# Routed experts on the rows that chose them, in tiles of 128 rows, instead of every expert on every row

## The chip, the cores and the metric

One core of one Trainium2 chip. The metric is the device time of one execution in microseconds (us), median of three runs. TensorE is PE in the rows below, VectorE is DVE, ScalarE ACT, GpSimd POOL, SyncE SP.

## What is computed

One transformer layer on x of 4 x 2048 rows of 256 numbers, all fp32: layer norm with modulation, a delta-rule attention with convolutions and a learned mix of three branches, then the expert layer that the change is about. Only the last part of the reference matters here:

```
scores = jax.nn.sigmoid(x @ gate_weight.T)             # 16 experts in 4 groups
...                                                    # best 2 groups, then the best 4 experts of a row
combine = jnp.zeros((T, E), jnp.float32).at[jnp.arange(T)[:, None], topk_idx].add(topk_w)
up = jnp.einsum('th,ehi->eti', x, expert_up)           # 256 -> 128, per expert
down = jnp.einsum('eti,eih->eth', jax.nn.silu(up), expert_down)
moe_out = jnp.einsum('te,eth->th', combine, down)
shared = jax.nn.silu(x @ shared_up) @ shared_down      # 256 -> 512 -> 256
return (moe_out + shared).reshape(B, S, H)
```

12 of a row's 16 weights in `combine` are zero.

## The kernel before

The program runs seven stages one after the other, each a block of its own on all engines: setup, norm_inputs, conv_heads, long_filter, chunk_inverses, delta_scan and mix_and_experts. Only the last one is changed in substance (L1462 to L2082). It takes 16 units of 512 rows (UT; J = 4 pieces of 128 rows; UB = 4 units to a batch element).

For each unit there are two kinds of work. `mix(u, i, s)` has 40 numbered steps s on every engine: statistics of the three branches (DVE, s 0 and 1, L1873; POOL takes the square roots as powers, L1655), the router network (PE s 7 to 15, L1697 to L1718; ACT gelu L1805), softmax (s 15 to 17), the weighted sum of the branches (DVE L1922 to L1934, POOL L1660 and L1663), its rms (ACT L1812, DVE L1937, POOL L1666, DVE L1943), the output projection (PE s 29 and 30, L1725 and L1732), the residual x2 (DVE L1952), its layer norm (L1958 to L1968, POOL L1668), transposes and modulation to h2T (PE L1740, ACT L1826), and the gate logits (PE s 38, L1746; ACT exp L1831). `route` (DVE, four parts, L1979 to L2044) makes the weights `comb` from them. Each step waits for the one before it, mostly on another engine, so a unit's mix is one chain.

The expert part has NX = 20 slots per unit: 4 pieces of the shared expert and 16 routed experts. In a slot PE does `up` (L1755, two matmuls of 512 columns), ACT the silu (L1838), PE `down` (L1769, four matmuls of 256 columns), and DVE adds the result times its weight into `acc` (L2060). All 16 experts run on all rows, whatever the weights; their up and down weights stay in SBUF (`eup`, `edn`).

`units_ahead` (L240) orders it: `front` runs the mix of unit 0 alone, then each `body` of unit u writes its 20 slots and the mix of unit u+1 interleaved, two steps a slot, in the same fixed order on every engine. The bodies are a hardware loop over three batch elements and a tail. Every engine is in order. The mix inputs vf, fl, dl, x and hT are double buffered and loaded on SP's queue; POOL closes a unit with `finish` (L1673, L1676), and SP stores it.

An fp32 matmul stands twice in the trace (x8 for four matmuls).

## Time and profile before

| what | value |
|---|---|
| median of three runs | 3187.55 us (3185.85 to 3205.73) |
| the profiled execution | 3187.41 us, span 3185.6 us |
| PE busy in the span | 88% |
| DVE, ACT, POOL busy | 52%, 34%, 19% |
| granted PE clock, mean | 0.817 of 2.4 GHz |
| bytes moved by DMA | 269.81 MB, 85 GB/s |

Busy is the time in which an engine had an instruction under way; it says nothing of what would be late next if that engine were faster. The granted clock is 1.00 at 2.4 GHz and 0.50 at 1.2 GHz; a value between is a mean over a stretch. The span is the first to the last instruction; the time of the execution is 1.8 us longer.

### The profile page before, as it was taken

What the parts mean: (1) busy time and instruction counts of PE and PEld (TensorE: products, weight loads), DVE (VectorE), ACT (ScalarE), POOL (GpSimd) and SP (SyncE); (2) the same over time, 40 slices, a digit from 0 to 9 for tenths busy, and PEclk for the clock granted to TensorE, in tenths of its full rate; (3) what the DMA queues carried; (4) which work ended last, traced back from release to release, by engine and by line L of the source; (5) the groups of instructions that cost most, each with busy time, mean ns of one, the idle gap of its engine ahead of it and who ended that gap; (6) DMA issues with size and microseconds to landing.
All of it is one profiled execution on the core that took longest, in us unless ns stands there. A gap on an engine that the chain in (4) does not pass through costs nothing.

```text
span 3185.6 us, 39962 instructions
## 1 busy us (share of the span) xinstructions
PE 2801.9 (88%) x13712; PEld 2052.0 (64%) x13712; DVE 1650.9 (52%) x4322; ACT 1076.5 (34%) x2142; POOL 618.1 (19%) x417
## 2 busy tenths in 40 slices
PE   4989994444998799999569999999999999999998
PEld 4966663333888678788446666666666666666665
DVE  3448883218142233333246665675656756667655
ACT  1258774233543111111123333323333233333231
POOL 1115552021100100000122122221222212222201
PEclk7579997665555666665679999999999999999999
DMA  3425557765663433434410011110111101111000
GB/s 97 139 93 164 162 172 194 184 131 129 148 140 103 136 108 109 129 87 129 159 40 19 29 47 47 48 47 1 47 47 48 47 1 47 47 47 47 7 1 14
DMA packets 348447, 269.81 MB, mean 85 GB/s; under 512 B 166284, under 2 KB 305996, under 8 KB 346724
## 3 DMA queue, kind: packets, MB, share of 16 engines
q1 hardware_dynamic: 337680, 256.90, 27.9%
q0 software_dynamic: 2304, 8.39, 1.0%
q10 hardware_dynamic: 8276, 2.10, 0.3%
q8 instruction: 108, 1.77, 0.2%
q14 instruction: 79, 0.65, 0.1%
HBM read 166.45 MB, written 100.89 MB: 84 GB/s over the span
## 4 chain that ended last, share of the span: by engine, by line
PE 35%; DVE 7%; POOL 6%; issue 2%; SPq 0%; DMA 0%; ACT 0%; POOLq 0%; DVEq 0%; ACTq 0%
PE mx_dn L1769 12%; PE mx_up L1755 11%; PE mx_m L1708 4%; POOL mx_st L1655 3%; DVE mx_acc L2060 3%; PE mx_m L1709 2%; PE mx_m L1717 2%; PE mx_m L1732 2%; POOL mx_rms L1666 1%; DVE mx_t L1922 1%; PE mx_m L1746 1%; POOL mx_acc L1673 1%; PE mx_m L1718 1%; POOL mx_acc L1676 1%; DVE mx_t L1943 1%
## 5 line engine op out<-in xcount | busy, mean ns | idle before, releaser
L2060 DVE SCALAR_TENSOR_TENSOR mx_acc<-mx_dn,mx_comb,mx_acc 128x256 f32<-128x256 f32 x1024 | 424.4, 477 | 476.5 <-PE mx_dn L1769 474.4
L1769 PE MATMUL mx_dn<-mx_edn,mx_hs 128*128 128x256 f32 x2048 | 513.3, 395 | 3.2 <-ACT mx_hs L1838 3.2
L1769 PEld LDWEIGHTS mx_dn<-mx_edn,mx_hs 128*128 128x128 f32 x2048 | 398.0, 197 | 168.2 <-issue 95.0
L1755 PE MATMUL mx_up<-mx_h2T,mx_eup 128*128 128x512 f32 x1024 | 496.2, 608 | 0.0
L1838 ACT ACTIVATE mx_hs<-mx_up 128x512 f32<-128x512 f32 x320 | 190.0, 596 | 789.8 <-PE mx_up L1755 789.5
L1755 PEld LDWEIGHTS mx_up<-mx_h2T,mx_eup 128*128 128x128 f32 x1024 | 189.2, 192 | 156.2 <-issue 147.0
L652 DVE SCALAR_TENSOR_TENSOR cv_acc<-cv_pre,conv_w,cv_acc 128x512 f32<-128x512 f32 x288 | 215.7, 750 | 88.8 <-ACT cv_acc L574 82.0
L516 PE MATMUL cv_pj<-cv_hT,wqkv 128*128 128x512 f32 x384 | 182.2, 605 | 13.4 <-ACT cv_acc L574 7.3
L1442 ACT ACTIVATE ds_U<-ds_ups 64x256 f32<-64x256 f32 x64 | 24.1, 377 | 419.0 <-PE ds_ups L1335 419.0
L1660 POOL TENSOR_TENSOR mx_t<-mx_vf,mx_ids 128x1024 f32<-128x1024 f32 x16 | 31.5, 1966 | 645.9 <-DVE mx_pr L1917 645.9
L1195 DVE TENSOR_TENSOR ci_prod<-ci_Ad,ci_T 128x62 f32<-128x62 f32 (+15 forms) x124 | 67.0, 540 | 148.9 <-DMA ci_Ad<-diag_d 144.6
L806 PE MATMUL fl_ps<-fl_toep,fl_vc 128*84 128x98 f32 x512 | 58.1, 285 | 94.1 <-DMA fl_toep<-taps_d 50.3
L1088 PE MATMUL ci_yps<-ci_low,ci_A 128*96 128x64 f32 x512 | 98.3, 374 | 48.2 <-DMA ci_half<-invT_d 48.2
L1655 POOL TENSOR_TENSOR mx_st<-mx_tmp,root_pow 128x24 f32<-128x24 f32 x32 | 132.9, 4168 | 34.9 <-DVE mx_tmp L1888 34.9
L686 POOL TENSOR_TENSOR rn<-cv_ss,half_pow 128x8 f32 x64 | 129.0, 2016 | 11.6 <-POOL cv_ss L682 11.6
L1088 PEld LDWEIGHTS ci_yps<-ci_low,ci_A 128*96 128x96 f32 x512 | 86.5, 274 | 59.3 <-DMA ci_half<-invT_d 48.7
L1769 PEld LDWEIGHTS mx_dn<-mx_sdn,mx_hs 128*128 128x128 f32 x512 | 97.3, 190 | 40.5 <-issue 30.5
L1708 PE MATMUL mx_m<-mx_hT,wr 128*128 128x512 f32 x256 | 122.1, 600 | 0.8 <-ACT mx_stT L1798 0.8
L1755 PE MATMUL mx_up<-mx_h2T,mx_sup 128*128 128x512 f32 x256 | 120.0, 602 | 1.6 <-issue 1.6
L1769 PE MATMUL mx_dn<-mx_sdn,mx_hs 128*128 128x256 f32 x512 | 121.0, 379 | 0.0
L1300 POOL TENSOR_TENSOR ds_v<-ds_v,rb 128x256 f32<-128x256 f32 x64 | 38.3, 629 | 418.5 <-DMA ds_k<-k_d 418.5
L806 PEld LDWEIGHTS fl_ps<-fl_toep,fl_vc 128*84 128x84 f32 x512 | 56.1, 185 | 96.0 <-DMA fl_toep<-taps_d 51.3
(227 smaller groups left out, 4783.9 us busy)
## 6 DMA issues: line engine op xcount, KB each, us to landing
kqT_d<-cv_kqc SPq DMA_DIRECT2D x16, 1024.0 KB, 8.0
vf_d<-cv_vf SPq DMA_DIRECT2D x16, 1024.0 KB, 5.3
ds_kqT<-kqT_d SPq DMA_DIRECT2D x16, 1024.0 KB, 5.8
mx_vf<-vf_d SPq DMA_DIRECT2D x16, 1024.0 KB, 6.2
fl_toep<-taps_d SPq DMA_DIRECT2D x32, 392.0 KB, 5.1
fl_pool<-vf_d SPq DMA_DIRECT2D x8, 1216.0 KB
xin<-_attn_hidden_states_dram SPq DMA_DIRECT2D x16, 512.0 KB, 3.8
hT_d<-hT SPq DMA_DIRECT2D x16, 512.0 KB, 2.6
```

The lines of the kernel that those rows point to most:

```text
L516: ins = pe.matmul(pj[o % 2][:], m.wqkv[:, k, weight(o) * P:(weight(o) + 1) * P], hT[i][:, k, :], start=(k == 0), stop=(k == KD - 1))
L652: ins = dve.scalar_tensor_tensor(out=acc[o % 3][:], in0=pre[i][:, o, t:t + UT], scalar=m.conv_w[:, weight(o), t:t + 1], in1=acc[o % 3][:], ...
L686: pool.tensor_tensor(m.rn[:, bass.ds(u * (J * 2 * H) + j * 2 * H, 2 * H)], ss[j % 2][:], m.half_pow[:, 0:2 * H], ALU.pow).then_inc(rn_done, 1)
L806: ins = pe.matmul(ps[r][0:NA, c // 4, (c % 4) * WIN:(c % 4 + 1) * WIN], vc[:, ch, :], toep[q][:, n * CB + c, ::-1], start=True, stop=True)
L1088: ins = pe.matmul(y_ps[x % 2][0:K3, h * DK:(h + 1) * DK], A[t % (RA // B)][:, b, h, 0:K3], low[t % RB][:, b * H + h, :], start=True, stop= ...
L1195: dve.tensor_tensor(o, Ad[q][:, :, c:, j:j + 1].to_broadcast([P, 2, k, c]), T[q][:, :, j:j + 1, 0:c].to_broadcast([P, 2, k, c]), ALU.mult) ...
L1655: pool.tensor_tensor(std[:, :, 1, :], tmp[:, 2, part].rearrange("p (a h) -> p a h", h=H), m.root_pow[:, part].rearrange("p (a h) -> p a h" ...
L1708: pe.matmul(out[:], m.wr1[:, k, f * P:(f + 1) * P], hT[i][:, k, :], start=(k == 0), stop=False)
L1755: ins = pe.matmul(up_ps[x % 2][:], lhs, h2T[i][:, k, :], start=(k == 0), stop=(k == KD - 1))
L1769: ins = pe.matmul(dn_ps[(i + n) % 2][:, j, :], hs[x % 4][:, j * P:(j + 1) * P], rhs, start=(x == 0 and j % 2 == 0) or x >= NS, stop=(x >= ...
L1838: act.activation(hs[x % 4][:], up_ps[x % 2][:], ACT.Silu).then_inc(silu_done, 1)
L2060: ins = dve.scalar_tensor_tensor(out=acc[i][:, j, :], in0=dn_ps[(i + n) % 2][:, j, :], scalar=comb[i][:, j, e:e + 1], in1=acc[i][:, j, :], ...
```

## The change

The routed experts run only on the rows that chose them. A unit no longer has 16 expert slots. Instead:

- `rank` (DVE, with `count` on PE) gives each chosen (row, expert) pair a place in a region of its expert in a DRAM tensor X_d; `scatter` (POOL, 16 indirect DMAs a unit) writes the normalised rows there.
- After the four units of a batch element, `tables` (DVE) computes how the filled regions are cut into tiles of 128 rows, NTL = 80 tiles a batch element (at most 64 full ones and a part tile for each of 16 experts); `pads` (SP) zeroes what follows each region, 16 writes at computed addresses.
- A tile then takes: its 128 rows loaded from X_d (SP, `xload`, address read from a table in SBUF), its expert's up weights fetched from DRAM on ACT's queue (`load_up`, address read the same way), two transposes (`turn`), modulation (ACT, `modulate`), up (`raise_`), silu, down (`lower`, with an expert number that PE reads from the table), a copy out of PSUM by ACT or DVE in turn, and a store to Y_d.
- Two batch elements later `gather` (POOL, 16 indirect DMAs a unit) fetches each row's four results, and `total` (DVE) adds them, with their weights, to the shared part and x2, which went through DRAM (sh_d, x2_d).

So there are B + 2 = 6 rounds of four bodies: round 0 has mix, shared expert and scatter, round 1 tiles of batch element 0 beside that, rounds 2 and 3 gathers too, round 4 tiles and gathers without mix, round 5 gathers alone. A body has NX = 24 slots: 4 shared, 20 with one tile each; the 40 steps of mix are spread over the 24. The bodies are written out, not looped. The mix inputs, x2, h2T and acc have one buffer now. The stage no longer holds `eup` in SBUF, and PE's first wait covers only the shared weights; `edn` comes later. `m.setup_sems` becomes `m.used_sems`, cleared by POOL a stage earlier, and four tensors of the middle stages are freed before the last.

```diff
+    NTL = 80
+    NQ = B * NTL
+    PER = NTL // UB
+    NX = NS + PER
+    STEPS = 40
...
+        def steps(x):
+            return range(x * STEPS // NX, (x + 1) * STEPS // NX)
...
+            def pads(b):
+                sp.wait_ge(tab_done, b + 1)
+                if b >= 2:
+                    sp.wait_ge(xT_done, NTL * (b - 1))
+                for e in range(E):
+                    r = sp.value_load(tab_p[b % 2][0:1, e:e + 1], min_val=0, max_val=2 * ROWS - P)
+                    sp.dma_start(m.X_d[bass.ds(r, P), :], zrow[:]).then_inc(pad_out, 16)
...
+            def xload(n):
+                b, t = n // NTL, n % NTL
+                r = sp.value_load(tab_s[b % 2][0:1, t:t + 1], min_val=0, max_val=2 * ROWS - P)
+                if n >= 4:
+                    sp.wait_ge(xT_done, n - 3)
+                sp.dma_start(xt[n % 4][:], m.X_d[bass.ds(r, P), :]).then_inc(xt_in[n % 4], 16)
+            def ystore(n):
+                b, t = n // NTL, n % NTL
+                if t == 0 and b >= 2:
+                    sp.wait_ge(sum_done, TB * (b - 1))
+                sp.wait_ge(yt_done[n % 2], n // 2 + 1)
+                sp.dma_start(m.Y_d[b % 2][t * P:(t + 1) * P, :], yt[n % 4][:]).then_inc(yt_out[b % 2][n % 4], 16)
...
+            for b, g, u in bodies():
+                v = u - 2 * UB
+                for x in range(NX):
+                    n = u * PER - NTL + x - NS
+                    if 1 <= b <= B:
+                        if g == 0 and x == NS - 1:
+                            batch_ready(b - 1)
+                            xload(n + 1)
+                            xload(n + 2)
+                        if x >= NS:
+                            if (n + 2) % NTL >= 2:
+                                xload(n + 2)
+                            if n >= 3:
+                                ystore(n - 3)
+                    if b >= 2:
...
+            def scatter(u, j):
+                b = u // UB
+                pool.wait_ge(place_done, u + 1)
+                if u % UB == 0 and j == 0 and b >= 1:
+                    pool.wait_ge(xT_done, NTL * (b - 1) + 1)
+                for k in range(TOPK):
+                    n = column(u, j, k)
+                    pool.indirect_dma_start(m.X_d[:, :], bass.IndirectOffsetOnAxis(ap=idx[b % 2][:, n:n + 1], axis=0),
+                                            xn[u % 2][:, j * D:(j + 1) * D], None).then_inc(scat[u % 2], 16)
+            def gather(v, j):
+                b, n = v // UB, v * J + j
+                if v % UB == 0 and j == 0:
+                    pool.wait_ge(idy_done, b + 1)
+                    for r in range(4):
+                        pool.wait_ge(yt_out[b % 2][r], 16 * NTL // 4 * (b // 2 + 1))
+                if n >= 2:
+                    pool.wait_ge(sum_done, n - 1)
+                for k in range(TOPK):
+                    c = column(v, j, k)
+                    pool.indirect_dma_start(G[n % 2][:, k, :], None, m.Y_d[b % 2][:, :],
+                                            bass.IndirectOffsetOnAxis(ap=idy[b % 3][:, c:c + 1], axis=0))\
+                        .then_inc(G_in[n % 2], 16)
...
+                if more_mix:
+                    deviations(u + 1)
+                if b >= 2:
+                    gather(v, 0)
+                    gather(v, 1)
+                if more_mix:
+                    products(u + 1)
+                if b >= 2:
+                    gather(v, 2)
+                if b < B:
+                    scatter(u, 0)
+                    scatter(u, 1)
+                if more_mix:
+                    rms_root(u + 1)
+                if b >= 2:
+                    gather(v, 3)
+                if b < B:
+                    scatter(u, 2)
+                    scatter(u, 3)
+                if more_mix:
+                    ln_root(u + 1)
...
+            def turn(n):
+                b, t = n // NTL, n % NTL
+                if t == 0:
+                    pe.wait_ge(tab_done, b + 1)
+                expert[n] = pe.value_load(tab_e[b % 2][0:1, t:t + 1], min_val=0, max_val=E - 1)
+                pe.wait_ge(xt_in[n % 4], 16 * (n // 4 + 1))
+                if n >= 2:
+                    pe.wait_ge(hTt_done, n - 1)
+                if n % PER == 0:
+                    pe.wait_ge(sh_ev, min(NU, n // PER + UB + 1))
+                for k in range(KD):
+                    ins = pe.transpose(xT_ps[n % 2][:, k * P:(k + 1) * P], xt[n % 4][:, k * P:(k + 1) * P], m.ident[:])
+                ins.then_inc(xT_done, 1)
+            def raise_(n):
+                pe.wait_ge(hTt_done, n + 1)
+                pe.wait_ge(eup_in[n % 4], 16 * (n // 4 + 1))
+                if n >= 2:
+                    pe.wait_ge(tsilu_done, n - 1)
+                if n == 0:
+                    pe.wait_ge(e_in, 16)
+                for k in range(KD):
+                    ins = pe.matmul(up_ps[n % 2][:, 0:P], eup[n % 4][:, k, :], hTt[n % 2][:, k, :],
+                                    start=(k == 0), stop=(k == KD - 1))
+                ins.then_inc(tup_done, 1)
+            def lower(n):
+                pe.wait_ge(tsilu_done, n + 1)
+                if n >= 2:
+                    pe.wait_ge(yt_done[n % 2], n // 2)
+                pe.matmul(dn_ps[n % 2][:, 0:D], hst[n % 2][:], edn[:, bass.ds(expert[n], 1), :].squeeze(1),
+                          start=True, stop=True).then_inc(tdn_done, 1)
+            pe.wait_ge(w_in, 16 * 2)
+            pe.wait_ge(const_done, 14)
+            for s in range(STEPS):
+                mix(0, s)
...
+            def load_up(n):
+                b, t = n // NTL, n % NTL
+                act.wait_ge(tab_done, b + 1)
+                e = act.value_load(tab_e[b % 2][0:1, t:t + 1], min_val=0, max_val=E - 1)
+                if n >= 4:
+                    act.wait_ge(tup_done, n - 3)
+                act.dma_start(eup[n % 4][:], w.expert_up[bass.ds(e, 1)].squeeze(0).rearrange("(k p) i -> p k i", p=P))\
+                    .then_inc(eup_in[n % 4], 16)
...
+            def modulate(n):
+                b = n // NTL
+                act.wait_ge(xT_done, n + 1)
+                if n >= 2:
+                    act.wait_ge(tup_done, n - 1)
+                for k in range(KD):
+                    ins = act.activation(hTt[n % 2][:, k, :], xT_ps[n % 2][:, k * P:(k + 1) * P], ACT.Identity,
+                                         scale=m.mod[:, 8 + k, b:b + 1], bias=m.mod[:, 6 + k, b:b + 1])
+                ins.then_inc(hTt_done, 1)
...
+            def tile_silu(n):
+                act.wait_ge(tup_done, n + 1)
+                if n >= 2:
+                    act.wait_ge(tdn_done, n - 1)
+                act.activation(hst[n % 2][:], up_ps[n % 2][:, 0:P], ACT.Silu).then_inc(tsilu_done, 1)
...
-                if e == 0:
-                    dve.wait_ge(comb_done, u + 1)
-                dve.wait_ge(dn_done, u * NX + (NS + e + 5))
-                if e == 0:
-                    dve.wait_ge(sh_ev, u + 1)
+            def rank(u):
+                b, g = u // UB, u % UB
+                n = u * 8
+                wide = lambda a: a.unsqueeze(2).to_broadcast([P, J, TOPK, E])
+                cols = slice(g * J * TOPK, (g + 1) * J * TOPK)
+                if g == 0:
+                    dve.tensor_scalar(run[:], first[:, b % 2, :], 1.0, None, ALU.mult).then_inc(rank_step, 1)
                 else:
-                    dve.wait_ge(dn_ev, u * E + (e + 2))
-                for j in range(J):
...
+            def total(v, j):
+                b, n = v // UB, v * J + j
+                q = n % 2
+                s = n * 5
+                dve.wait_ge(G_in[q], 16 * TOPK * (n // 2 + 1))
+                dve.wait_ge(c_in[q], 32 * (n // 2 + 1))
+                for k in range(TOPK):
...
+                v = u - 2 * UB
                 for x in range(NX):
-                    if x >= NS:
-                        expert(u, i, x - NS)
-                    if nxt is not None:
-                        mix(nxt, 1 - i, 2 * x)
-                        mix(nxt, 1 - i, 2 * x + 1)
-                    if x < NS:
-                        route(u, i, x)
-            dve.wait_ge(const_done, 4)
```

PE, in the last stage: a piece of one body before, with names as in the text (mx_eup and mx_edn are the routed weights, mx_m is a PSUM bank of the mix):

```order
L1708 MATMUL mx_m<-mx_hT,wr 128x512 x2
L1709 MATMUL mx_m<-mx_stT,wr1s 128x512
L1755 MATMUL mx_up<-mx_h2T,mx_eup 128x512 x2
L1760 REGISTER_ALU
L1765 REGISTER_ALU
L1769 MATMUL mx_dn<-mx_edn,mx_hs 128x256 x4
L1755 MATMUL mx_up<-mx_h2T,mx_eup 128x512 x2
```

The same place now, a slot of a tile between two pieces of the router network (mx_tab_e is the table of expert numbers, mx_xt the tile's rows):

```order
L1905 MATMUL mx_m<-mx_stT,wr1s 128x512
L1987 TENSOR_LOAD mx_tab_e
L1987 ISA x2
L1994 MATMUL mx_sh<-ident,mx_xt 128x128 x2
L2005 MATMUL mx_up<-mx_hTt,mx_eup 128x128 x2
L2013 ISA
L2013 MATMUL mx_dn<-mx_edn,mx_hst 128x256
L1904 MATMUL mx_m<-mx_hT,wr 128x512 x2
```

The six matmuls of 512 and 256 columns in a routed slot became five with 128 and 256 columns, and a read of a register from SBUF stands ahead of them.

ACT, a slot of a tile in the last stage now (before, this was one row, `L1838 ACTIVATE mx_hs<-mx_up 128x512`); x_d is the DRAM copy of x2:

```order
L2076 DMA x_d<-mx_x 128x1024
L2109 TENSOR_LOAD mx_tab_e
L2109 ISA x2
L2112 ISA
L2112 DMA mx_eup<-in_L_ffn_expert_up_dram 128x2x128
L2121 ACTIVATE mx_hTt<-mx_sh,mod 128x128 x2
L2129 ACTIVATE mx_hst<-mx_up 128x128
L2135 ACTIVATE mx_yt<-mx_dn 128x256
```

A register read and a DMA issue are now in ACT's queue ahead of each tile's activations. L2135 stands in every second slot.

POOL, one whole body before:

```order
L1655 TENSOR_TENSOR mx_st<-mx_tmp,root_pow 128x6x4 x2
L1660 TENSOR_TENSOR mx_t<-mx_vf,mx_ids 128x1024
L1663 TENSOR_TENSOR mx_t<-mx_vf,mx_pr 128x1024
L1666 TENSOR_TENSOR mx_rms<-mx_rms,half_pow 128x16
L1668 TENSOR_TENSOR mx_rstd<-mx_mv,half_pow 128x4
L1673 TENSOR_TENSOR mx_acc<-mx_acc,gbB 128x1024
L1676 TENSOR_TENSOR mx_acc<-mx_acc,mx_x 128x1024
```

POOL, one whole body of round 2 or 3 now (mx_G<-Y_d are gathers, X_d<-mx_xn are scatters):

```order
L1808 TENSOR_TENSOR mx_st<-mx_tmp,root_pow 128x6x4 x2
L1848 DMA mx_G<-Y_d,mx_idy 128x256 x8
L1814 TENSOR_TENSOR mx_t<-mx_vf,mx_ids 128x1024
L1817 TENSOR_TENSOR mx_t<-mx_vf,mx_pr 128x1024
L1848 DMA mx_G<-Y_d,mx_idy 128x256 x4
L1835 DMA X_d<-mx_xn,mx_idx 73984x256 x8
L1822 TENSOR_TENSOR mx_rms<-mx_rms,half_pow 128x16
L1848 DMA mx_G<-Y_d,mx_idy 128x256 x4
L1835 DMA X_d<-mx_xn,mx_idx 73984x256 x8
L1826 TENSOR_TENSOR mx_rstd<-mx_mv,half_pow 128x4
```

The two powers of the mix chain, mx_rms and mx_rstd, stand behind 12 indirect DMAs each (8 in rounds 0 and 1).

## Rows read from the trace of the kernel before

**Rows 1.** The last stage in three stretches: front, bodies, last body.
```profile
core 0: us, PE busy (x) PEld busy (x) DVE busy (x) ACT busy (x) POOL busy (x), PEclk, DMA share, GB/s
1548.00:1641.00 93.00, 35.12 (x116) 23.08 (x117) 32.37 (x142) 10.04 (x14) 21.47 (x11) 0.60 0.51 163
1641.00:3110.00 1469.00, 1455.52 (x5351) 942.05 (x5351) 922.63 (x2746) 497.23 (x663) 304.97 (x119) 0.97 0.10 34
```

**Rows 2.** Groups of the last stage: busy us, mean ns | idle before, releaser.
```profile
L1769 PE MATMUL mx_dn<-mx_edn,mx_hs 128*128 128x256 f32 x2048 | 513.3, 395 | 3.2 <-ACT mx_hs L1838 3.2
L1755 PE MATMUL mx_up<-mx_h2T,mx_eup 128*128 128x512 f32 x1024 | 496.2, 608 | 0.0
L2060 DVE SCALAR_TENSOR_TENSOR mx_acc<-mx_dn,mx_comb,mx_acc 128x256 f32<-128x256 f32 x1024 | 424.4, 477 | 476.5 <-PE mx_dn L1769 474.4 <-DVE mx_comb L2044 0.9
L1838 ACT ACTIVATE mx_hs<-mx_up 128x512 f32<-128x512 f32 x320 | 190.0, 596 | 789.8 <-PE mx_up L1755 789.5
```

**Rows 3.** The chain that ended last: the same step of two units, twelve units apart.
```profile
1905.66 2.91 POOL mx_rms L1666
...
3079.78 2.91 POOL mx_rms L1666
```

**Rows 4.** Timeline of the front (mix of unit 0 alone): start us, us.
```profile
1562.99 0.60 DVE L1873 BATCH_NORM_STATS2 mx_bs<-mx_vf 128x6 f32<-128x64 f32 x4 [16.94 <-DMA mx_hT<-hT_d]
...
1567.18 8.35 POOL L1655 TENSOR_TENSOR mx_st<-mx_tmp,root_pow 128x24 f32<-128x24 f32 x2 [15.19 <-DVE mx_tmp L1888]
...
1579.06 1.03 PE L1697 MATMUL mx_m<-ident,mx_st 128*24 128x128 f32 x4 [32.78 <-DMA mx_edn<-n_L_ffn_expert_down_dram]
...
1605.68 2.92 DVE L1924 TENSOR_TENSOR mx_t<-mx_dl,mx_pr 128x1024 f32<-128x1024 f32 x1
...
1616.61 2.90 POOL L1666 TENSOR_TENSOR mx_rms<-mx_rms,half_pow 128x16 f32<-128x16 f32 x1 [6.23 <-DVE mx_rms L1940]
...
1623.48 5.97 PE L1732 MATMUL mx_m<-wog,mx_oT 128*128 128x256 f32 x16 [0.69 <-ACT mx_oT L1816]
...
1641.26 0.22 ACT L1831 ACTIVATE mx_sc<-mx_m 128x64 f32<-128x64 f32 x1 [3.68 <-PE mx_m L1746]
```

**Rows 5.** Timeline inside a later body: start us, us.
```profile
2006.55 1.09 PE L1725 MATMUL mx_m<-ident,mx_t 128*128 128x128 f32 x8
...
2009.20 3.62 PE L1732 MATMUL mx_m<-wog,mx_oT 128*128 x16
...
2025.66 1.85 PE L1746 MATMUL mx_m<-wgT,mx_h2T 128*128 128x16 f32 x16
```

**Rows 6.** Groups of the last stage that bound the new operations.
```profile
L1826 ACT ACTIVATE mx_h2T<-mx_m,mx_modb 128x512 f32<-128x512 f32 x30 | 21.7, 773 | 25.3 <-PE mx_m L1740 25.3
...
L2020 DVE TENSOR_TENSOR mx_hm<-mx_ms 128x1024 f32<-128x1024 f32 x16 | 19.6, 1224 | 0.5
...
L1854 ACT ACTIVATE mx_acc<-mx_dn 128x1024 f32<-128x1024 f32 x16 | 16.3, 1020 | 0.0
...
L1999 DVE TENSOR_TENSOR mx_gq<-mx_gs 128x64 f32<-128x64 f32 x16 | 3.6, 225 | 0.6
...
L1831 ACT ACTIVATE mx_sc<-mx_m 128x64 f32<-128x64 f32 x16 | 3.6, 223 | 26.5 <-PE mx_m L1746 26.5
```

**Rows 7.** POOL's DMAs in stage chunk_inverses: busy us, mean ns.
```profile
L1024 POOL DMA_DIRECT2D ci_kT<-kqT_d x16 | 12.3, 769 | 296.6 <-POOLq L703 170.9 <-PE ci_gps L1076 125.6
```

**Rows 8.** SP's queue instructions for mx_vf: ns min/median/max.
```profile
L1608 SPq DMA_DIRECT2D mx_vf<-vf_d x16: 372/373/3506, 1551.2 to 2920.0; - x16
...
L1608 SPq MOVE mx_vf<-vf_d x14: 29/29/29, 1630.3 to 2920.0; - x14
```

**Rows 9.** DMA issues: KB each, median us from issue to landing.
```profile
mx_hT<-hT_d SPq DMA_DIRECT2D x16, 512.0 KB, 9.2
...
ci_half<-invT_d SPq DMA_DIRECT2D x64, 64.0 KB, 2.3
...
cT<-in_L_c_dram SPq DMA_DIRECT2D x8, 0.5 KB, 2.0
```

**Rows 10.** DMA in two stretches; columns as in rows 1.
```profile
100.00:1500.00 1400.00, 1142.47 (x7416) 948.71 (x7417) 599.96 (x1160) 531.38 (x1379) 270.00 (x258) 0.68 0.49 136
1570.00:1580.00 10.00, 0.94 (x4) 0.41 (x4) 1.01 (x8) 0.00 (x0) 5.52 (x2) 0.50 1.08 342
```

634 lines of the change are left out of this document (446 added, 188 removed).

## The prediction

> **What bounds the kernel now.** I read the windows of the last stage first, since only that stage changes. In its bodies PE is busy for 1455.5 of 1469 us at a granted clock of 0.97, so near its 2.4 GHz level; DMA is idle to nine tenths [rows 1]. The groups say what PE does: the routed experts' two lines hold 513 + 496 = 1009 us of it, and the engines beside it wait for it: DVE 474 us before the accumulations, ACT 790 us before the silus [rows 2]. The chain of waits repeats one step twelve units apart, so a body with mix takes (3079.78 - 1905.66)/12 = 97.8 us, PE bound [rows 3].
>
> The second thing to read is what PE's load hides. In the front the mix of unit 0 runs alone, and the timeline shows its chain from the first statistics (1562.99) to the gate's exp (1641.26): 78.3 us [rows 4]. 3.5 us of that is PE waiting for the expert weights until 1579.06, though POOL's powers were done at 1567.18 + 8.35 = 1575.5. So 74.8 us is what a unit's mix costs by latency alone, against 97.8 us for a whole body. The experts' 1009 us cannot all be won: below about 75 us a body is bound by the mix chain. And there are now 24 bodies, not 16.
>
> **What goes.** Per unit 16 slots of one up and one down, which are 1009/256 = 3.9 us each by busy time (with the overlap of two groups somewhat less), so about 60 us of PE; 64 DVE accumulations of 0.477 us [rows 2], which PE hid; 16 silus of 0.6 us. The front no longer waits for the routed weights: -3.5 us, so bodies begin at 1641.3 - 3.5 = 1638 [rows 4].
>
> **A tile's slot.** On ACT: two Identities of 128 columns lie between 0.22 (64 wide) and 0.77 (512 wide) [rows 6]; by the slope, some 0.65 for both; silu 0.28; half of a 256-wide copy 0.2; a DMA issue of 0.4 by SP's 0.37 [rows 8]. Then the register read from SBUF, which no row shows. Its bounds are a register move, 0.03 [rows 8], and the landing of the smallest transfer, 2.0 [rows 9], since it too fetches data before its queue can go on. I take the middle, 1.0. With 0.2 for waits that is 2.7 us. PE's share: 1.0 for its own read, two transposes 0.3 (8 in 1.09), four half matmuls for up 0.5 (16 narrow ones in 1.85), down 0.5 (16 in 3.62) [rows 5], 2.3 in all. So ACT sets a free-running slot: 2.7, between 1.7 and 3.7 by the bounds.
>
> The Trainium skill has a price for that read: "DMA: Bandwidth & Descriptors", section "Latency and other measured facts", gives a floor of about 600 ns for a tensor_load. No row here shows one. The sum below would be some 110 us lower by it.
>
> **Round 0: mix, shared expert, scatter.** The chain's 74.8, plus: the shared expert's four slots stand ahead of the first transposes, about 17 us against 12.6 for the statistics and powers, +4.5; the copy and DRAM store of the shared part stand in ACT ahead of the next step, 1.0 [rows 6] + 0.5; `rank` on DVE after the branch products, some ten small operations between 0.22 and 1.22 [rows 6], +2.8; the scatters. POOL has eight of them between its products and mx_rms. The nearest row is its direct DMA of 128 rows, 0.77 each [rows 7]; no gather or scatter is shown, so 0.75 below, and above 2.0, the smallest landing [rows 9], were each to wait for its indices. I take 1.0: 8 us, of which DVE's sums, the square and the reduction cover 5, +2.9. The eight ahead of mx_rstd lie beside the output projection (5.97) and layer norm [rows 4]. Sum 86.5, say 86. Single buffers: the loads start at x2 and take 9.2 to land [rows 9], about what remains of the chain, 0. Once a batch element `tables` runs on DVE, thirty operations of 0.2 to 1.3, 12 us on the chain. Round 0: 4 x 86 + 12 = 356.
>
> **Round 1: tiles too.** All engines pass the 24 slots in one order, and a tile's copy ties DVE and ACT to PE within two slots, so tiles hide only where the mix chain waits on others. Between softmax and the transposes of t3 (slots 10 to 17) it waits some 20 us for DVE, POOL and ACT: eight slots of 2.3 hide there. In slots 4 to 9 PE itself is the chain (router network): 6 x 2.2 = 13. In slots 18 to 23 there are another 13, with some 5 hidden under layer norm: 8. So +20, 106 a body. `pads` puts 16 register reads and issues, 16 x 1.4 = 22 us, into SP's queue ahead of the tile loads and stores; two to four tiles are ahead, so half is felt: 12. Round 1: 4 x 106 + 12 + 12 = 448.
>
> **Rounds 2 and 3: gathers too.** One `total` (six DVE operations around 0.45, 2.7 [rows 2]) falls before the sums, and four more gathers lie ahead of each power, mostly covered: +5, 111 a body. Seven bodies with mix, one pair of tables and pads: 7 x 111 + 24 = 801. The last has no mix: 17 + 20 x 2.7 + 24 for tables and pads = 95.
>
> **Rounds 4 and 5.** 4 x 20 x 2.7 + 5 for the scatters to land = 221. Then gathers alone, two buffers: a piece's four issues (4.0) + landing (2.3 to 2.5 [rows 9]) + total (2.7), two in flight, 4.6 a piece, 16 of them, + 8 for draining the tiles = 82.
>
> **Sum.** 1638 + 356 + 448 + 801 + 95 + 221 + 82 = 3641; the execution lies 1.8 above its span: 3643 us, against 3187.41 of the profiled execution, which is the median (3187.55) within 0.2. That is 14% slower. Half of PE's work is gone, and the body is longer.
>
> DMA: a full body moves 3.1 MB of loads, 7.9 for tiles (three times 131 KB, 20 times), 4.2 of scatter and gather, 3.1 of shared, x2 and output, 18.3 MB in all. With large rows the engines gave 342 GB/s when full; with small ones 136 at a share of 0.49, so 278 [rows 10]. 66 us at 278, below 111: hidden, if the landings don't stretch.
>
> **Clock.** Where PE was busy a third of the time (the front) its granted clock was 0.60, and 16 matmuls of the projection took 5.97 us; in the bodies, at 0.97, 3.62 [rows 1, 4, 5]. PE is busy for half of a round-0 body, so I used the front's times. Were the clock high, transposes, projection and gate would give back 7 us a body.
>
> **Rivals.**
> *The tiles vanish into the chain (faster).* If the register read costs like a move (slot 1.7) and tiles, tables and pads all run inside the waits of a 75 us chain: 1638 + 15 x 75 + (17 + 34) + 4 x 34 + 62 = 3012, + 1.8 = 3014 us. For it: the chain was measured, and POOL, DVE and ACT have half their time free. Against it: the in-order slots, and rank and scatters inside the chain. With those tail prices it decides at a mean body of (3185.6 - 1638 - 51 - 136 - 62)/15 = 86.6 us; above that it is slower.
> *Cheap slots.* Read 0.03, everything else as forecast: 1.0 less in 12 exposed slots of 11 bodies (132), rounds 4 (80), the last mix-less body (20) and pads (40): 3371 us. For it: nothing in the trace speaks against a fast read.
> *POOL is the bound.* Indirect DMAs at 2.0: the eight ahead of mx_rms cost 8 more in 15 bodies, the twelve ahead of mx_rstd overrun by 4 in 11, and the tail's pieces 4 more in 16: 120 + 44 + 64: 3871 us. For it: when POOL and DVE run together the trace has a DVE product at 2.92 for 1.22 [rows 4, 6], so the two hinder each other. [...]
> *DMA bound.* Indexed 1 KB rows run at half the rate of small rows here: 18.3 MB at 139 GB/s is 132 us in eleven bodies: +231, 3874 us.
>
> **How the numbers follow.** Forecast 0.52; cheap slots 0.20; POOL 0.12; DMA 0.05; tiles vanish 0.07; between these two last signs, within 1% of before (which is about what a measurement of this kernel can tell from no change), 0.04. So faster 0.07, same 0.04, slower 0.89. Range: the register read's bounds are -270 and +270 around 3643, the issue's -46 and +228. From 3330, below the cheap slots, to 3900, above POOL and DMA; what is left out is the faster and the equal case and the sum of two bad ones.
>
> **What would show it.** Right: PE's share of the last stage near half; mean body of round 0 near 86 and of rounds 2 and 3 near 111; ACT in round 4 one tile in 2.7 us with a gap of a microsecond before each pair of Identities; POOL's mx_rms starting right behind eight scatters. Wrong: a register read well under 0.5 us, a round-0 body near 75, PE still above 90% busy, or a DMA share near 1 in rounds 2 and 3.

## The result, and the profile after

The changed kernel takes 3655.3 us (median of four, 3642 to 3672) against 3196.6 for the kernel before on the same chip: ratio 1.143, 95% interval 1.135 to 1.151, 14% slower. The forecast was 3643, range 3330 to 3900. The profiled execution spans 3648.1 us.

The page after: its first line, busy times, PE's row in 40 slices, the clock, the DMA share, and three queues.

```profile
span 3648.1 us, 46279 instructions
...
PE 2565.8 (70%) x13360; PEld 1988.7 (55%) x13360; DVE 1571.8 (43%) x4122; ACT 1261.8 (35%) x2962; POOL 1112.8 (31%) x907
...
PE   5989954459989889936665778747777477764660
...
PEclk7599976655556666766776778876787677777885
DMA  3345567646533333242212344444455444555785
...
q1 hardware_dynamic: 461584, 368.37, 33.8%
q0 software_dynamic: 26880, 75.53, 6.9%
```

The last stage begins in the 18th slice. Before, PE was busy for nearly all of its bodies [rows 1]; now it stands mostly at 6 or 7 (4 where a round ends, 0 when the tiles are done), no other engine is above 5 until the last slice (POOL 6), and DMA rises to 8 only at the end. No engine is full, so the order of waits must set most of the time; the experiments below test that. The windows of the three stretches with mix, and two of the end, answer to [rows 1]:

```profile
1644.00:1995.00 351.00, 205.55 (x698) 137.44 (x697) 170.04 (x558) 59.46 (x80) 142.14 (x88) 0.70 0.23 79
1995.00:2444.00 449.00, 323.72 (x1329) 233.38 (x1329) 183.76 (x597) 186.71 (x386) 142.07 (x88) 0.77 0.39 126
2444.00:3257.00 813.00, 580.57 (x2343) 426.74 (x2343) 388.06 (x1193) 327.96 (x679) 373.85 (x274) 0.75 0.51 158
...
3400.00:3450.00 50.00, 33.65 (x175) 24.16 (x173) 17.35 (x39) 24.21 (x74) 16.44 (x18) 0.90 0.85 255
...
3550.00:3600.00 50.00, 0.00 (x0) 0.00 (x0) 22.24 (x48) 0.00 (x0) 36.20 (x36) 0.52 0.52 151
```

PE is busy for 59% of round 0, 72% of round 1 and 71% of rounds 2 and 3, at clocks of 0.70 to 0.77 (before: 0.97). The two routed lines, 1009 us in [rows 2], have become these groups:

```profile
L2121 ACT ACTIVATE mx_hTt<-mx_sh,mod 128x128 f32<-128x128 f32 x640 | 257.7, 454 | 462.8 <-PE mx_sh L1994 246.3
L2013 PE MATMUL mx_dn<-mx_edn,mx_hst 128*128 x640 | 265.8, 507 | 166.7 <-DVE mx_yt L2444 120.4
L1848 POOL DMA_INDIRECT mx_G<-Y_d,mx_idy x256 | 267.5, 1045 | 280.9 <-DVE mx_co L2461 127.3
L2005 PE MATMUL mx_up<-mx_hTt,mx_eup 128*128 128x128 f32 x1280 | 264.3, 343 | 99.6 <-ACT mx_hTt L2121 74.5
L1835 POOL DMA_INDIRECT X_d<-mx_xn,mx_idx x256 | 268.6, 1049 | 112.5 <-issue 74.6
```

That is 530 us of matmuls in place of 1009, and 169 us more for the tiles' transposes (L1994, 640 of them). What was saved came back as waits. The length of a body is read from the gate's exp, once per unit:

```profile
L2088 ACT ACTIVATE mx_sc<-mx_m x16: 223/223/224, 1644.0 to 3257.3; 128x64 f32<-128x64 f32 x16
```

The 15 intervals between these 16 starts (from the timeline) are 85.2, 86.2, 85.1, 94.5 | 112.2, 104.7, 105.9, 126.4 | 113.3, 110.3, 111.8, 136.4, 111.6, 111.3, 118.4. "Tail" below is from the last of them, 3257.3, to the span's end. All runs by these stretches, in us:

```
run              chip  front    r0     r1    r2,3   tail    span
forecast               1638    356    448    801    398    3641
changed kernel    a    1644.0  351.0  449.1  813.1  390.8  3648.1
e_static          b    1638.8  352.3  430.7  795.8  369.6  3587.2
e_notile          b    1669.0  355.9  351.1  652.6  242.2  3270.8
e_scatter_late    b    1665.4  368.0  440.6  796.5  401.1  3671.6
e_load_early      b    1660.9  351.1  433.6  787.6  389.7  3623.0
e_scatter_split   b    1644.2  350.5  436.1  852.7  385.3  3668.8
e_rank_late       b    1653.8  334.3  430.0  824.8  380.7  3623.5
e_steps           b    1648.1  350.6  408.8  779.1  389.0  3575.5
e_tail            b    1654.5  351.5  444.0  815.1  389.3  3654.4
e_gather_first    c    1653.1  330.8  413.4  731.5  362.9  3491.6
e_warm            c    1655.7  350.9  437.9  772.7  364.3  3581.6
e_combined        c    1636.6  321.9  400.5  747.0  366.4  3472.4
e_loads_spread    d    1649.5  328.2  404.1  776.1  383.5  3541.5
```

The stretches are those of the one profiled execution of each run. The front is the same code nearly everywhere and varies by 32 us, more than several edits are worth, so edits are compared by stretches. Runs with one of the letters b, c and d ran on the same chip; on which chip the changed kernel's own run (a) stood is not known, but e_tail shows nearly its stretches on chip b. The kernel before took 3195 and 3218 us on chip b at two times, and 3199 and 3197 on c and d. The letters matter (see e_warm). Of the last run's four executions one took 4026.8 us at a granted clock of 0.56 and is left out of its median.

### The profile page after: what moved, and what is told of

The parts are those of the page before. It is cut to its first block, busy times and chain, and to the rows that moved or that the text cites. A ratio compares the mean times of both kernels' runs of the same rounds, so it can differ in the third digit from the quotient of the medians.

```text
span 3648.1 us, 46279 instructions
## 1 busy us (share of the span) xinstructions
PE 2565.8 (70%) x13360; PEld 1988.7 (55%) x13360; DVE 1571.8 (43%) x4122; ACT 1261.8 (35%) x2962; POOL 1112.8 (31%) x907
## 3 DMA queue, kind: packets, MB, share of 16 engines
q1 hardware_dynamic: 461584, 368.37, 33.8%
## 4 chain that ended last, share of the span: by engine, by line
issue 13%; PE 10%; DVE 9%; POOL 8%; SPq 7%; DMA 6%; ACT 2%; another core or an unknown queue 1%; ACTq 1%; POOLq 0%; DVEq 0%
DMA mx_hT<-hT_d 4%; POOL mx_G L1848 3%; POOL X_d L1835 2%; DVE mx_bs L2179 2%; PE mx_m L1913 2%; PE mx_m L1904 2%; SPq L1712 1%; POOL mx_st L1808 1%; DMA mx_xt<-X_d 1%; POOL mx_rms L1822 1%; PE mx_dn L2013 1%; SPq L1715 1%; PE mx_up L2005 1%; SPq L1722 1%
## 5 line engine op out<-in xcount | busy, mean ns | idle before, releaser
L2121 ACT ACTIVATE mx_hTt<-mx_sh,mod 128x128 f32<-128x128 f32 x640 | 257.7, 454 | 462.8 <-PE mx_sh L1994 246.3
L2013 PE MATMUL mx_dn<-mx_edn,mx_hst 128*128 x640 | 265.8, 507 | 166.7 <-DVE mx_yt L2444 120.4
L1848 POOL DMA_INDIRECT mx_G<-Y_d,mx_idy x256 | 267.5, 1045 | 280.9 <-DVE mx_co L2461 127.3
L2005 PE MATMUL mx_up<-mx_hTt,mx_eup 128*128 128x128 f32 x1280 | 264.3, 343 | 99.6 <-ACT mx_hTt L2121 74.5
L1835 POOL DMA_INDIRECT X_d<-mx_xn,mx_idx x256 | 268.6, 1049 | 112.5 <-issue 74.6
L2005 PEld LDWEIGHTS mx_up<-mx_hTt,mx_eup 128*128 128x128 f32 x1280 | 231.1, 254 | 115.6 <-ACT mx_hTt L2121 86.3
L1994 PE MATMUL mx_sh<-ident,mx_xt 128*128 128x128 f32 x640 | 168.6, 355 | 149.2 <-DMA mx_xt<-X_d 121.5
L1994 PEld LDWEIGHTS mx_sh<-ident,mx_xt 128*128 128x128 f32 x640 | 94.8, 177 | 254.5 <-DMA mx_xt<-X_d 162.2
L2013 PEld LDWEIGHTS mx_dn<-mx_edn,mx_hst 128*128 128x128 f32 x640 | 132.3, 256 | 176.5 <-issue 176.5
L2456 DVE SCALAR_TENSOR_TENSOR mx_co<-mx_G,mx_wts,mx_co 128x256 f32<-128x256 f32 x256 | 124.0, 484 | 71.1 <-DMA mx_G<-Y_d,mx_idy 38.8
```

Of the source, the lines that this page charges most:

```text
L1835: pool.indirect_dma_start(m.X_d[:, :], bass.IndirectOffsetOnAxis(ap=idx[b % 2][:, n:n + 1], axis=0), xn[u % 2][:, j * D:(j + 1) * D], None ...
L1848: pool.indirect_dma_start(G[n % 2][:, k, :], None, m.Y_d[b % 2][:, :], bass.IndirectOffsetOnAxis(ap=idy[b % 3][:, c:c + 1], axis=0))\
L1994: ins = pe.transpose(xT_ps[n % 2][:, k * P:(k + 1) * P], xt[n % 4][:, k * P:(k + 1) * P], m.ident[:])
L2005: ins = pe.matmul(up_ps[n % 2][:, 0:P], eup[n % 4][:, k, :], hTt[n % 2][:, k, :], start=(k == 0), stop=(k == KD - 1))
L2013: pe.matmul(dn_ps[n % 2][:, 0:D], hst[n % 2][:], edn[:, bass.ds(expert[n], 1), :].squeeze(1), start=True, stop=True).then_inc(tdn_done, 1)
L2121: ins = act.activation(hTt[n % 2][:, k, :], xT_ps[n % 2][:, k * P:(k + 1) * P], ACT.Identity, scale=m.mod[:, 8 + k, b:b + 1], bias=m.mod[: ...
```

## Experiments

The diffs are cuts: each shows lines that carry its edit, not all of them.

**Tiles left out.** Every tile's instructions and the pads are gone; Y is zeroed once.

```diff
-                    if 1 <= b <= B and x >= NS:
+                    if False:
                         turn(n)
```

> All work on tiles is left out: their loads, the padding, transposes, products, silus, copies and stores; Y is set to zero once in round 0. Router, scatter, tables, gathers and totals stay. Theory A (the forecast's): the mix chain sets the bare body, and tiles add 20 us to it. Then a body of round 1 is as long as one of round 0, 85 to 86 us, one of rounds 2 and 3 some 91 (5 for totals and gathers), the last of a round 12 more for the tables; rounds 4 and 5 are bare sums, 16 pieces of 5.4 us each, 87 each: near 1644 + 351 + 356 + 649 + 30 + 87 + 87 = 3204 us. Rival B (loads, gathers and totals, not tiles, stretch the bodies): bodies of rounds 2 and 3 stay at 100 us or more without tiles. Rival C (in-order engines hide nothing): bodies of round 1 fall by all 20 slots of 2.2 us, to 62, below the front's chain of 75.

Measured 3260.9 us (ratio 1.021, 1.011 to 1.031). Round 1 took 351.1 us, no longer than round 0 (355.9), and rounds 2 and 3 652.6 (649 expected). So A: the mix chain sets the bare body, and tiles add (449.1 - 351.1)/4 = 24.5 and (813.1 - 652.6)/7 = 22.9 us to it, pads included. It also prices the rest: tables +10.3 in a round's last body, totals and gathers +6.5 a body. The tail came to 242, not 204: gathers are dearer than I had them. And with no tile at all it is still no faster than the kernel before: the chain and the two draining rounds eat the whole gain.

What the tiles bring is not PE's work alone, and one part of it stands in no term of the forecast. ACT loads a table of functions each time that it goes from the mix's gelu or exp to a tile's silu and back (changed kernel; busy us, mean ns | idle before):

```profile
L2129 ACT ACT_TABLE_LOAD x44 | 56.5, 1283 | 0.8
L2062 ACT ACT_TABLE_LOAD x38 | 48.8, 1283 | 35.4 <-DVE mx_comb L2352 35.0
```

There are 10 such loads in a body of rounds 1 to 3, and 3 in round 0 and in every body without tiles: 7 x 1.28 = 9.0 us of ACT's time a body come with the tiles. The kernel before had ten a body too, beside a PE that was busy for 99% of its bodies. How much of the 9.0 us is felt no run isolates.

**Register reads.**

```diff
-                e = act.value_load(tab_e[b % 2][0:1, t:t + 1], min_val=0, max_val=E - 1)
+                e = t // 4 % E
```

> A fixed expert and a fixed row of the regions for every tile, instead of the numbers read from the tables (PE, ACT and SP read no register in a tile; the pads keep theirs). It leaves out the choice of the tiles by the counts, and nothing else of the work: as many tiles, loads, products and stores. The profile after shows the read itself at 0.28 to 0.30 us, not the 1.0 us of my forecast. Theory A (the sum's accounting with the measured size): each read is felt once in the 12 exposed slots of 11 bodies, in the 80 slots of round 4 and in the 20 of the last body without mix, 232 slots at 0.3 us, so -70 us, near 3585 us. Theory B (the reads lie in waits for other things, SP's loads and DVE's copies): less than 15 us. Theory C (the read costs what I put into the sum, with a stall behind it that its own row does not show): -230 us, near 3420 us.

The rows of the changed kernel (ns min/median/max) show the read and the arithmetic on its result:

```profile
L2109 ACTq TENSOR_LOAD <-mx_tab_e x320: 275/282/911, 2012.6 to 3540.8; - x160
...
L1712 SPq TENSOR_LOAD <-mx_tab_s x320: 4/270/1137, 1988.3 to 3540.3; - x160
...
L1987 PEldq TENSOR_LOAD <-mx_tab_e x320: 296/302/942, 2008.4 to 3543.3; - x160
L1987 PEldq FUSED_REGOPS  x320: 146/146/165, 2008.9 to 3543.7; - x160
```

Measured 3584.7 us, -71 by the medians where theory A had -70. That match is in part luck, since the front helped: by stretches it is -18 in round 1, -17 in rounds 2 and 3 and -21 in the tail, 57 in all. Read and arithmetic are about 0.45 us an engine and tile; over the 232 slots that theory A counts, 57 us are 0.25 a slot, so about half of it is felt.

**Scatters and rank.** Three runs move POOL's scatters behind the two powers; the first puts all 16 behind mx_rstd.

```diff
-                    scatter(u, 0)
-                    scatter(u, 1)
                 if more_mix:
                     rms_root(u + 1)
...
                     ln_root(u + 1)
+                if b < B:
+                    for j in range(J):
+                        scatter(u, j)
```

> POOL issues all 16 scatters of a unit behind the power of the layer norm (mx_rstd) instead of eight ahead of mx_rms and eight ahead of mx_rstd; all of the work is kept. Theory A (the forecast's term): the eight ahead of mx_rms cost the chain 2.9 us in each of 15 bodies, at the measured 1.27 us apiece rather 5, so bodies of round 0 fall from 85.2 to 80 to 82 us and the whole by 45 to 75 us. Rival B: they lie beside the square and the reduction on ACT and DVE, and nothing changes (within 10 us). Rival C: the 16 together now delay the powers of the next unit's deviations at the body's start, and the bodies grow.

Measured 3662.5 us: nothing in sum. The timelines show both halves of it. The changed kernel, POOL from the second branch product on, then two rows of DVE, the second of which mx_rms needs:

```profile
1774.00 2.90 POOL L1817 TENSOR_TENSOR mx_t<-mx_vf,mx_pr 128x1024 f32<-128x1024 f32 x1
1780.81 1.77 POOL L1835 DMA_INDIRECT X_d<-mx_xn,mx_idx  x1 [3.90 <-DVE mx_idx L2384]
1782.88 0.96 POOL L1835 DMA_INDIRECT X_d<-mx_xn,mx_idx  x1 [0.30 <-issue]
...
1791.45 2.94 POOL L1822 TENSOR_TENSOR mx_rms<-mx_rms,half_pow 128x16 f32<-128x16 f32 x1
...
1780.43 1.22 DVE L2238 TENSOR_TENSOR mx_t<-mx_t 128x1024 f32<-128x1024 f32 x1
...
1785.28 0.17 DVE L2246 TENSOR_SCALAR mx_rms<-mx_rms 128x16 f32<-128x16 f32 x1
```

and the first run, first body:

```profile
1707.52 2.90 POOL L1817 TENSOR_TENSOR mx_t<-mx_vf,mx_pr 128x1024 f32<-128x1024 f32 x1
1719.25 2.90 POOL L1822 TENSOR_TENSOR mx_rms<-mx_rms,half_pow 128x16 f32<-128x16 f32 x1 [8.84 <-DVE mx_rms L2243]
```

DVE's sum is there at 1785.45 and mx_rms starts at 1791.45: eight scatters, 0.96 + 0.30 us each, hold it 6 us. With them away that body took 78.4 us. But the 16 then stood ahead of the next unit's deviations, which began 13.6 us behind the exp in the second body (1757.47) instead of 6.6, and the following bodies took 95.5, 89.2 and 104.8: rival C beside A. Hence the split, eight behind each power:

```diff
                 if more_mix:
                     rms_root(u + 1)
+                if b < B:
+                    scatter(u, 0)
+                    scatter(u, 1)
                 if more_mix:
                     ln_root(u + 1)
+                if b < B:
+                    scatter(u, 2)
+                    scatter(u, 3)
+                if b >= 2:
+                    gather(v, 3)
```

> POOL issues eight of a unit's scatters behind mx_rms and eight behind mx_rstd (the changed kernel: eight ahead of each); nothing is left out. With all 16 behind mx_rstd, the first body of round 0 fell to 78.4 us, since mx_rms then waited 8.8 us for DVE's sum alone instead of 14.5 us, but the next ones took 89 to 95 us: POOL reached the next unit's deviations late. Theory A (what stands ahead of mx_rms is on the chain, and between mx_rms and mx_rstd there are 15 us free for eight scatters of 1.27): every body of round 0 takes 79 to 80 us, those of rounds 1 to 3 fall by 3 to 5, in all 60 to 80 us less, near 3590 us. Rival B (the gain of the first body was only the scatters' late start, and the next wait takes it): no body below 84 us.

Measured 3659.3. The second and third body of round 0 took 81.5 us for 85 to 86, but the first took 88.3 and the fourth 99.1, so round 0 as a whole stayed at 350.5. Round 1 lost 13, and rounds 2 and 3 grew by 40. A holds for single bodies, not in sum. And with rank later:

```diff
-                    if b < B and x == 11:
+                    if b < B and x == 16:
                         rank(u)
```

> As the run with the scatters split, and DVE also does rank (and at a round's end the tables) in slot 16, behind the product with mx_rms, instead of slot 11, between the branch products and their sums; nothing is left out. Theory A (the forecast's terms: rank 2.8 us on the chain of each body, tables 10 to 12 us at a round's end): bodies 2.8 us shorter than with the scatters split alone, 77 in round 0, and the last body of a round some 6 us less, since tables then lie beside the output projection's 6 us: another 45 to 60 us off. Rival B (rank lies beside POOL's branch products, which end after it): less than 10 us. Rival C (PE's transposes now wait for rank's read of the counts, and the scatters start later and meet the next deviations): longer.

Measured 3626.0: the first three bodies of round 0 took 80.2 (5.3 less than in the changed kernel; rank's share is 1.4, half of its 2.6 us), and a round's last body lost 14 us in round 1 against the split. Rounds 2 and 3 were still 12 longer. A row of DVE in the split run says why: I had also moved the fourth piece's gathers behind the scatters.

```profile
2548.15 1.01 DVE L2456 SCALAR_TENSOR_TENSOR mx_co<-mx_G,mx_wts,mx_co 128x256 f32<-128x256 f32 x2 [18.99 <-DMA mx_G<-Y_d,mx_idy]
```

DVE sits 19 us before that total, and the layer norm of the mix is queued behind it. In the run with rank late such waits add up to 113.6 us, one in each of the seven bodies. The next run puts the gathers back in front:

```diff
                     rms_root(u + 1)
+                if b >= 2:
+                    gather(v, 3)
                 if b < B:
                     scatter(u, 0)
```

> As the run with rank in slot 16 and the scatters behind the powers, but the gathers of the fourth piece stand ahead of the scatters again (behind mx_rms, as in the changed kernel); nothing is left out. In the two runs before, rounds 0 and 1 fell by 14 (scatters split) and 36 us (rank too), while rounds 2 and 3 grew by 40 and 12. Theory A (DVE's total of the fourth piece stands in slot 20 ahead of the layer norm of the mix, so it holds the chain until the gathers have landed, and I had put these behind 16 scatters of 1.27 us): the seven bodies of rounds 2 and 3, 825 us then, fall to 785 to 800, below the changed kernel's 813, and the whole is 50 to 65 us under the changed kernel's 3655. Rival B (POOL's total work, 32 indexed transfers of 1.27 us and 18 us of powers and products in a body, is what stretches rounds 2 and 3): they stay at 820 or more.

Measured 3496.1 us (ratio 1.093, 1.088 to 1.098). Rounds 2 and 3 fell to 731.5, 41 below the same stretch of e_warm on the same chip, where it is the changed kernel's code. A holds, and by more than its 13 to 28 us: POOL does the same work, only the order differs. DVE's wait before the totals is no longer among its long ones.

**Loads released early.**

```diff
-                if u:
-                    sp.wait_ge(x2_done, 2 * u)
+                if u:
+                    sp.wait_ge(pool_mix, 2 * u)
+                    sp.wait_ge(mix_step, 4 * u - 2)
                 sp.dma_start(vf[:], m.vf_d[rows].rearrange("j p c -> p j c")).then_inc(loaded[i], 16)
```

> The next unit's loads are released one by one: hT after the router network's last product, vf, fl and dl after the branch products have read them, only x after x2, each with a semaphore of its own; all of the work is kept. I had put the exposure of the loads at 0; the profile after shows the first statistics 2.6 us behind the gate's exp in round 0 and a DVE wait of about 8 us for hT's landing in a body of round 3. Theory A: these waits are on the chain, so -2.6 us in 4 bodies and -5 to -8 in 11: -65 to -95 us in all. Rival B: the exposed time is taken by the next wait (the shared expert's four slots stand ahead of the transposes anyway), under 15 us. Rival C: the loads' issues stand further ahead in SP's queue and hold back tile loads behind their waits: bodies of rounds 1 to 3 grow.

Measured 3608.5: -15.5 in round 1, -25.5 in rounds 2 and 3, nothing in round 0 (A in the later ones, at half to three quarters of its size; B in round 0). POOL's rows of the changed kernel's second body (begins 1729.20), then of this run's (begins 1745.7, 1660.9 + 84.8):

```profile
1735.80 4.16 POOL L1808 TENSOR_TENSOR mx_st<-mx_tmp,root_pow 128x24 f32<-128x24 f32 x1 [14.54 <-DVE mx_tmp L2194]
...
1771.10 2.94 POOL L1814 TENSOR_TENSOR mx_t<-mx_vf,mx_ids 128x1024 f32<-128x1024 f32 x1 [25.25 <-DVE mx_pr L2223]
```

```profile
1743.30 4.16 POOL L1821 TENSOR_TENSOR mx_st<-mx_tmp,root_pow 128x24 f32<-128x24 f32 x1 [5.52 <-DVE mx_tmp L2207]
...
1787.62 2.94 POOL L1827 TENSOR_TENSOR mx_t<-mx_vf,mx_ids 128x1024 f32<-128x1024 f32 x1 [31.41 <-DVE mx_pr L2236]
```

The deviations came 9 us sooner (2.4 before the exp instead of 6.6 behind it), the branch product 41.9 us behind the exp in both: in round 0 PE still works on the shared expert's slots until 1745.1 in the changed kernel, and the router network stands behind them.

**Where the tiles stand.** The router network's steps in slots 4 to 6, softmax to transposes in 7 to 19.

```diff
-            return range(x * STEPS // NX, (x + 1) * STEPS // NX)
+            cuts = [0, 1, 3, 5, 7, 10, 13, 16, 17, 18, 19, 20, 21, 22, 23, 24, 25, 26, 27, 28, 29, 32, 35, 38, 40]
+            return range(cuts[x], cuts[x + 1])
```

> Another table of the mix steps over the slots: the router network's steps in slots 4 to 6 instead of 4 to 9, the steps from softmax to the output transposes one each in slots 7 to 19 (13 tiles beside them instead of eight), the last eleven steps in slots 20 to 23; nothing is left out. Theory A (the forecast's: a tile is felt where PE itself is the chain and hidden where the chain waits for others): five tiles fewer are felt, 5 x 2.2 = 11 us in each of 11 bodies, -120 us, near 3530 us; round 0 as before. Rival B (the tiles' copies keep DVE and ACT, in order, in step with PE, so a chain step waits for the tiles ahead of it wherever they stand): within 25 us of the changed kernel. Rival C (a longer stretch delays the output steps behind 13 tiles): 30 us or more longer.

Measured 3576.9 us, the best single edit in groups a and b that keeps all the work: -40 in round 1 and -34 in rounds 2 and 3, round 0 unchanged. A in direction, six tenths of its size: 6.8 us a body and not 11. The run does not separate A from another cause: with the router network in three slots instead of six ACT changes its table 8 times a body and not 10, which is 2 x 1.28 = 2.6 us less.

**The tail.** Tile rows three ahead, four buffers for gathered rows.

```diff
-                if n >= 2:
-                    pool.wait_ge(sum_done, n - 1)
+                if n >= 4:
+                    pool.wait_ge(sum_done, n - 3)
```

> Tile rows are loaded three tiles ahead instead of two (the four buffers stay), and the gathered rows have four buffers instead of two; nothing is left out. It acts on rounds 4 and 5, 391 us from the last gate's exp to the end. In round 4 PE waits 61 us for tile rows at 2.2 to 2.3 us a slot; in round 5 a piece takes 5.4 us and more for 5.1 of four gathers. Theory A (latency): round 4 falls by 25 to 45 us, the drain of round 5 by 10 to 20, rounds 1 to 3 by little: 35 to 65 us less. Rival B (transfers: the DMA engines are busy to 0.78 in round 4, and SP's issues are in order behind stores): less than 15 us. Rival C (POOL, running ahead with its gathers, is late for the mix powers in rounds 2 and 3): bodies there grow by 1 to 3 us.

Measured 3648.7, tail 389.3 for 390.8: B, in that a longer lead brings nothing. What limits round 4 stays open. The DMA engines are near full (share 0.86 from 3400 to 3500), but they are not at their limit: on the same chip, with as many tiles and bytes (from fixed addresses) and no register reads, e_static had a tail of 369.6 and this window (columns as in [rows 1]),

```profile
3368.00:3468.00 100.00, 68.64 (x398) 52.29 (x396) 37.62 (x85) 56.38 (x171) 38.51 (x40) 0.93 0.93 286
```

286 GB/s for 255. In round 5 it is POOL's issue rate. POOL's waits in 3560:3648, of the changed kernel and of this one (total us, times, longest):

```profile
POOL mx_G L1848 <- issue: 21.3, 55, 2.7
...
POOL mx_G L1848 <- DVE mx_co L2461: 3.4, 2, 2.5
```

```profile
POOL mx_G L1849 <- issue: 18.6, 61, 0.3
```

With four buffers POOL waits for nobody there, gathers follow each other in 1.3 us, and it ends no sooner.

**The clock.**

```diff
                         count(u)
+                    if b == 0 and x == 11:
+                        pe.wait_ge(sh_ev, u + 1)
+                        for _ in range(28):
+                            pe.matmul(xT_ps[0], sup[:, 0, 0:P], h2T[:, 0, :], start=True, stop=True, skip_group_check=True)
```

> In round 0 alone, 28 more matmuls of 512 columns, whose results nobody reads, stand in PE's 24 us of idle time between the counts and the output transposes; nothing is left out. It tests whether a low granted clock (0.70 in round 0) is part of the body. Theory A (PE idle for half of a body lowers its clock, and the chain's own matmuls pay): the granted clock of round 0 rises to 0.85 or more, the 16 matmuls of the output projection take 3.6 instead of 5.2 us, and each body of round 0 loses 2 to 5 us, 351 to near 338. Rival B (the clock rises, but PE's part of the chain after the gap is short): within 1 us a body. Rival C (the extra matmuls end after the product with mx_rms is ready, and delay the transposes): bodies longer by what overruns the gap.

The output projection's matmuls in round 0, changed kernel and this run (ns min/median/max), and this run's window:

```profile
L1930 PE MATMUL mx_m<-wog,mx_oT x64: 379/634/794, 1711.2 to 1982.8; 128*128 128x256 f32 x64
```

```profile
L1930 PE MATMUL mx_m<-wog,mx_oT x64: 379/379/793, 1724.0 to 1994.4; 128*128 128x256 f32 x64
```

```profile
1656.00:2007.00 351.00, 306.36 (x921) 179.99 (x921) 169.90 (x558) 59.26 (x81) 142.43 (x88) 0.84 0.23 79
...
1781.54 26.39 PE L2048 MATMUL mx_sh<-mx_h2T,mx_sup 128*128 128x512 f32 x56
```

The granted clock rose from 0.70 to 0.84 (means between its levels, 1.2 and 2.4 GHz), and the projection fell from 5.22 to 3.72 us and the transposes ahead of it from 1.97 to 1.04, yet round 0 took 350.9 us for 351.0: the extra matmuls needed 26.4 us, about 2 more than the gap, and gave back what they won. So the low clock costs some 2.4 us at this place of a body. The output transposes of the layer norm (1.97 us) and the gate (3.6 us) ran no faster than before, behind PE's next waits, so what the clock costs there is not tested.

The surprise is elsewhere. Rounds 1 to 5 of this run are the changed kernel's code, yet 3580.3 us is 75 less than 3655.3: -11, -40 and -26 by stretches. The other two runs on chip c have short tails too (362.9 and 366.4, where the runs on chip b with the register reads had 381 to 401), so it goes with the chip or the hour and not with the extra matmuls. On it, 100 us of round 4 moved more:

```profile
DMA packets 30116, 25.52 MB, mean 255 GB/s; under 512 B 3102, under 2 KB 28970, under 8 KB 30104
```

```profile
DMA packets 33376, 27.99 MB, mean 280 GB/s; under 512 B 3398, under 2 KB 32199, under 8 KB 33364
```

(the changed kernel from 3400, this run from 3360). The kernel before took 3197 us beside the changed kernel and 3199 beside this run. It is tempting to call the transfers of this chip faster, but the page of this run says otherwise for its largest queue:

```profile
q1 hardware_dynamic: 461584, 368.37, 34.5%
```

34.5% of 3581.6 us is 1236 us for 368.37 MB; in the changed kernel it was 33.8% of 3648.1, 1233 us for the same bytes. The engines took as long for a byte; in round 4 they were busy for 0.93 of the time instead of 0.86, as in e_static. Why they are kept busier on this chip, and what shortens rounds 1 to 3, is not known.

**All together.** Early loads, scatters and gathers as above, rank in slot 16, the step table, and pads two per slot:

```diff
-                for e in range(E):
+                for e in range(2 * (x - 16), 2 * (x - 15)):
                     r = sp.value_load(tab_p[b % 2][0:1, e:e + 1], min_val=0, max_val=2 * ROWS - P)
```

> All that helped, together: loads released one by one, scatters behind the powers with the fourth piece's gathers ahead of them, rank and tables in slot 16, the table of steps with 13 tiles between softmax and transposes, and the padding's 16 register reads and stores spread over eight slots, two each. Nothing is left out. Theory A (each acts on another wait, three quarters of the single gains stay): 75 from the steps, 42 from the loads, 50 from scatters and rank, 15 from the pads, times 0.75: 135 us less, near 3520. Rival B (all of them act on the same waits in rounds 1 to 3, so the best one alone remains): 3560 to 3580. Rival C, that it beats the kernel before at 3190 to 3220: it would need bodies of 80 us in rounds 1 to 3, which the run without any tiles did not reach in rounds 2 and 3 (91).

Measured 3479.5 us (ratio 1.089, 1.084 to 1.095): 101 below e_warm on its chip. That lies between A (135 less) and B (75 to 95 less): the scatter edit alone had 84 there, so early loads, step table and pads added 17 between them. Rounds 2 and 3 took 747, more than the 731.5 of the scatter edit alone. SP's queue and PE in one of those bodies:

```profile
2538.96 0.42 SPq L1697 DMA_DIRECT2D mx_vf<-vf_d  x1
2539.42 0.52 SPq L1698 DMA_DIRECT2D mx_fl<-fl_d  x1
2539.99 0.60 SPq L1699 DMA_DIRECT2D mx_dl<-o_d  x1
2541.33 4.68 SPq L1726 DMA_DIRECT2D mx_xt<-X_d  x1
```

```profile
2554.58 0.69 PE L2009 MATMUL mx_sh<-ident,mx_xt 128*128 128x128 f32 x2 [12.87 <-DMA mx_xt<-X_d]
```

The tile's row load stands behind 2.6 MB of unit loads (hT was issued at 2538.42), and PE waits 12.9 us for tile rows. Hence the last run:

```diff
-                    if x == 15 and u + 2 < NU:
-                        load(u + 2)
+                    if x in (9, 12, 14, 16, 18) and u + 2 < NU:
+                        load(u + 2, [(9, 12, 14, 16, 18).index(x)])
```

> As the combined run, but the 2.6 MB of a unit's early loads are issued in five pieces of 0.5 MB over slots 9 to 18 (hT, the two halves of vf, fl, dl) instead of together in slot 15; nothing is left out. In the combined run SP issued them within 2.2 us, the tile row load behind them took 4.7 us to issue, and PE then waited 12.9 us for the row, in every body of rounds 2 and 3 once. Theory A (a burst of 2.6 MB at 280 GB/s keeps the DMA engines for 9 us, and tiles with two tiles of lead cannot bridge that; pieces of 0.5 MB take 2 us each, which they can): the 12.9 us go, 8 or more of them come off a body, 11 bodies: -90 us, near 3390. Rival B (the bytes are the same and so is the time that they take from the tiles): within 20 us of the combined run's 3480. Rival C (SP now waits in slots 9 to 18 for the branch products before it can issue the next tile rows): longer. Rounds 4 and 5 are the same code in nearly all runs and serve as a mark of the chip's DMA rate: 389 us from the last gate's exp to the end in the first two calls, 364 in the third.

Measured 3543.2 (median of three, 3514 to 3546; ratio 1.104, 1.093 to 1.115) on a chip where the tail took 383.5, nearer to chip b's than to c's, so against 3479.5 it says little. PE's waits for tile rows in rounds 2 and 3, combined run and this one:

```profile
PE mx_sh L2009 <- DMA mx_xt<-X_d: 90.8, 22, 12.9
```

```profile
PE mx_sh L2016 <- DMA mx_xt<-X_d: 40.5, 22, 12.1
```

They fell by half, and the bodies did not follow (776.1; e_combined's 747 plus the 40 by which e_warm and the changed kernel differ would be 787). B, as far as this goes; it is not settled.

## Why the prediction was right, step by step

- **The bare chain.** Round 0 was forecast at 356 and took 351.0; with mix but no tiles the length stayed. Sizes inside were off: scatters 6 us late instead of 2.9 (1.26 apiece, not 1.0), with rank 5.3 us together where I had 5.7.
- **Signs.** Round 0 near 86 and rounds 2 and 3 near 111 came (85.5, and 112.8 in the bodies that don't end a round), and mx_rms started right behind its eight scatters. PE's share, meant to be near half, was 64% from 1644 on. A sign of being wrong came too, the register read well under 0.5 us. DMA's share in rounds 2 and 3 was 0.51, far from 1.
- **Clock.** The projection took 5.22 us in round 0 where I used 5.97. Of the 7 us a body that a high clock would give back, e_warm shows 2.4 and leaves the rest untested.
- **Loads hidden, 0: wrong.** DVE's waits in 2444:3257 have this row (us, times, longest):

```profile
DVE mx_bs L2179 <- DMA mx_hT<-hT_d: 62.2, 7, 10.5
```

  8.9 us a body, part of it beside the shared expert's slots; early release brought 3.6 to 3.9 a body. In round 0 the term was right.
- **Tiles +20 a body: right in sum** (21 to 22 without pads), **not in its parts.** It held 12 register reads at 1.0 us, and taking the reads out won 4.6 us a body in round 1 and 2.5 in rounds 2 and 3. Some 8 us of the 20 were thus something else. Candidates are PE's waits for copies and for tile rows, and ACT's 9.0 us of table loads, for which there was no term; no run says in what shares. That a tile's place matters was right: another table of steps brought 6.8 us a body. The pads' 12 measured 8.5 and 13.3 (a round's last body above the others, less the tables' 10.3), tables 10.3 for 12, totals and gathers 6.5 for 5.
- **Register read 1.0 us: wrong by half or more.** 0.27 to 0.30, some 0.45 with its register arithmetic. The Trainium skill's floor of about 600 ns ("DMA: Bandwidth & Descriptors", "Latency and other measured facts") is not borne out either: these rows lie at half of it.
- **Slot 2.7 in round 4: wrong.** It was 2.2 to 2.3 us from 3400 on. ACT was busy for 50 of 100 us there, and about 26 of its idle time ended with PE's transposes, which themselves waited for tile rows. Its own terms add to 2.1 us a slot (0.81 + 0.28 + 0.19 + 0.39 for the issue + 0.43 for the read), so it is not far from a bound either. 20 tiles and four pieces move 20 x 0.39 + 4 x 0.92 = 11.5 MB, 255 GB/s at that pace, and e_static shows that more was possible. From the first tile's transposes (3340.5) to the end of the last slot round 4 took about 206 us for 221.
- **Round 5: too small.** About 101 for 82; 5.2 us of POOL per piece instead of 4.0, and waits for totals.
- So 3641 against a span of 3648 is partly luck: u15's body (83 for 95), round 4 (-15) and round 0 (-5) gave 32 back, and the front (+6), rounds 1 to 3 (+13) and round 5 (+19) took them.

Of the rivals, the cheap read was true and its price still wrong: without any read the kernel takes 3585, not 3371, so about three quarters of that price were not there to win. What takes the read's place was not isolated. The tiles do not vanish. POOL as the bound at 2.0 us per transfer did not come: the two groups have means of 1.05. Single ones do take 1.8 to 2.0, as at 1780.81, where DVE's 1024-wide sum begins at 1780.43. Up to 3560 us 47 of 459 took more than 1.2 us, each beside a TENSOR_TENSOR of DVE, though not every one beside such an operation is long. The Trainium skill ("SBUF — State Buffer", "Who interferes with whom") says that a DVE instruction with two inputs in SBUF contends with a GpSimd instruction that reads SBUF; these rows agree with it, and the means hardly feel it. Indexed rows did not halve the DMA rate: with them in the mix the engines moved 255 to 280 GB/s.

## What to carry to other kernels

Saving the bound engine's work is worth only the distance to the next bound. Here that was a latency chain of 85 to 92 us against a body of 98, and the saving was paid for with two more rounds that nothing overlaps. Before such a change, time the chain alone and price the drain. And on in-order engines ask of every moved instruction what is queued behind its waits: POOL's scatters ahead of one power held a body by 6 us, and a total of DVE ahead of a layer norm by up to 19. Last, when different kinds of work are interleaved on ACT, count the table loads between them.

## What was not expected of the hardware

- A register read from SBUF took 0.27 to 0.30 us on PE, ACT and SP (medians of 320), plus 0.15 on PE for the arithmetic on it.
- An indexed transfer of 128 rows cost POOL 0.96 us and 0.30 until the next, whether scatter or gather (medians 0.95 and 0.97). Beside a TENSOR_TENSOR of DVE single ones took up to 2.0.
- Ten changes of ACT's function table in a body of rounds 1 to 3 took 12.8 us of its time, 1.28 each; three of them were there without tiles.
- Rounds 1 to 5 of the same program took 78 us less on chip c than in the changed kernel's own run, while the kernel before took the same time beside both. The DMA engines were busy for 0.93 instead of 0.86 of round 4 there, with no less time per byte; the cause is open.
- A 128 KB load issued behind 2.6 MB of others took 4.68 us to issue, where 0.35 is usual.
